# Graph attention and mixture of experts on one core: the transposes of a job's activations move between the two halves of an earlier job's second-layer product

## The reference, cut to what matters

```python
x = x + attention(layernorm(x), adj)        # 64 graphs, 128 nodes, 384 wide, 12 heads
u = layernorm(x)
logits = u.mean(nodes) @ router_w.T + router_b
top_v, top_i = top_k(logits, 2)             # 2 of 4 experts for each graph
gate = softmax(top_v)
h = act[e](u @ w1[e] + b1[e])               # act = gelu, silu, mish, gelu; 768 wide
out = h @ w2[e] + b2[e]
x = x + layernorm(gate-weighted sum of out + u)
```

## Time and profile before

| | |
|---|---|
| median of 3 runs | 1624.33 us (1623.05 to 1624.53) |
| the profiled execution's own time | 1624.39 us |
| its span in the trace | 1622.6 us |
| PE busy | 1587.3 us, 98% |
| DVE busy | 1195.4 us, 74% |
| ACT busy | 969.5 us, 60% |
| POOL busy | 686.8 us, 42% |
| matmul groups on L495 with `ut_in` (first layer) | x1536 and x768 |
| matmul groups on L495 with `at_hi`, `at_lo` (second layer) | x1524 and x762 |
| transposes on L709 | x768 |

### The profile page before, as it was taken

How to read it: one execution, slowest core, us unless ns; L and a number is a source line. 1 busy time by engine, 2 the same in 40 slices (tenths; PEclk the granted TensorE clock), 3 DMA queues, 4 the chain that set the end, 5 groups by cost and what they waited for, 6 DMA issues and landing times.

```text
span 1622.6 us, 44743 instructions
## 1 busy us (share of the span) xinstructions
PE 1587.3 (98%) x12720; PEld 1523.6 (94%) x12720; DVE 1195.4 (74%) x3754; ACT 969.5 (60%) x2880; POOL 686.8 (42%) x1105
## 2 busy tenths in 40 slices
PE   7999999999999999979999999999999999999998
PEld 7999999999999999869999999999999999999998
DVE  5787788878888788767766666776777767677776
ACT  6899999988889988853433333443444434343442
POOL 3777887778777787631111111111111111111112
PEclk9999999999999999999999999999999999999999
DMA  5433333344444433682111112211211111111211
GB/s 183 157 122 125 104 117 115 130 158 150 156 154 156 152 125 116 223 316 85 51 58 60 58 57 60 60 60 61 61 60 46 59 56 60 60 60 50 67 49 45
DMA packets 93511, 163.87 MB, mean 101 GB/s; under 512 B 10304, under 2 KB 73792, under 8 KB 92096
## 3 DMA queue, kind: packets, MB, share of 16 engines
q1 hardware_dynamic: 91664, 145.01, 27.3%
q10 hardware_dynamic: 1584, 15.73, 2.7%
HBM read 96.22 MB, written 64.49 MB: 99 GB/s over the span
## 4 chain that ended last, share of the span: by engine, by line
PE 89%; DVE 5%; ACT 2%; issue 2%; DMA 1%; DVEq 1%; POOL 0%; ACTq 0%; POOLq 0%; SPq 0%
PE bank L495 68%; PE bank L570 5%; PE bank L709 5%; PE bank L522 3%; PE bank L593 3%; PE bank L610 2%; PE bank L579 1%; PE bank L602 1%; DVE inverse L1461 1%; DVE half_t L1454 1%; DVE inverse L1457 1%; ACT inverse L1011 1%; ACT at_hi L1004 1%; DMA xu_scratch<-xu 1%; DVE hid L1335 0%
## 5 line engine op out<-in xcount | busy, mean ns | idle before, releaser
L495 PE MATMUL bank<-w_hi,ut_in 128*128 x1536 | 422.4, 342 | 0.4 <-issue 0.4
L495 PE MATMUL bank<-w_both,at_hi 128*128 x1524 | 388.6, 335 | 6.9 <-DVE at_lo L1426 6.2
L781 ACT ACTIVATE prob<-att,heads 128x128 f32<-128x128 f32 x768 | 297.7, 398 | 13.0 <-DVE heads L1178 10.8
L495 PEld LDWEIGHTS bank<-w_both,at_hi 128*128 128x128 f32 x1524 | 274.1, 188 | 12.5 <-issue 12.5
L495 PEld LDWEIGHTS bank<-w_hi,ut_in 128*128 128x128 f32 x1536 | 280.4, 189 | 1.4 <-issue 1.4
L495 PE MATMUL bank<-w_lo,ut_in 128*128 x768 | 257.6, 335 | 0.0
L495 PE MATMUL bank<-w_both,at_lo 128*128 x762 | 255.0, 335 | 0.0
L926 ACT ACTIVATE hid<-hid 128x384 f32<-128x384 f32 x192 | 95.0, 526 | 261.1 <-DVE hid L1335 256.2
L1004 ACT ACTIVATE at_hi<-bank,gate_col 128x384 fp32r<-128x384 f32 x254 | 133.7, 577 | 190.9 <-PE bank L709 189.0
L1154 POOL TENSOR_TENSOR xz<-xz,lnb_wide 128x384 f32<-128x384 f32 x64 | 68.0, 1063 | 405.9 <-DVE xz L1492 383.3
L1426 DVE SCALAR_TENSOR_TENSOR at_lo<-bank,gate_col,at_hi 128x384 fp32r<-128x384 f32 x254 | 144.7, 611 | 112.2 <-ACT at_hi L1004 112.2
(11 more groups left out here) (139 smaller groups left out, 3484.8 us busy)
## 6 DMA issues: line engine op xcount, KB each, us to landing
xu_scratch<-xu SPq DMA_DIRECT2D x64, 384.0 KB, 2.3
xz<-xu_scratch SPq DMA_DIRECT2D x64, 384.0 KB, 3.3
x_in<-in_x SPq DMA_DIRECT2D x32, 384.0 KB, 3.3
xu<-in_x SPq DMA_DIRECT2D x32, 384.0 KB, 4.4
ut_scratch<-ut_out SPq DMA_DIRECT2D x64, 192.0 KB, 1.9
ut_in<-ut_scratch SPq DMA_DIRECT2D x64, 192.0 KB, 2.3
out_dram<-xz SPq DMA_DIRECT2D x64, 192.0 KB, 1.9
w_lo<-in_L_ffn_w SPq DMA_DIRECT2D x4, 1152.0 KB, 6.6
```

The costliest lines, as they stand in the source:

```text
L495: last = nc.tensor.matmul(acc, lhs[c][a], rhs[c][b], start=start and n == 0, stop=stop and n == len(terms) - 1)
L781: nc.scalar.activation(prob[g][:, hh, :], att[g][:, head, :], ACT.Exp, bias=neg_max[g][:, head:head + 1], scale=-1.0, accum_out=row_sum[g] ...
```

## The change

In the second stage, PE's order becomes: at job j the first-layer product of j, the first half of the second-layer product of j - 2, the transposes of j - 1, the second half of the second-layer product of j - 2. ACT's second `at_hi` piece waits until the second-layer product of the job in front is over, since it overwrites what that reads. The transposes of the last job stand between the halves of job 126's product. The value loads that choose the experts (`choice`, L627) now stand one ahead of each product.

`half_t` moves to the memory of tiles `ot1` and `ot_hi1`, whose last reader is the last output projection (for which ACT waits there anyway), and `xz0` takes its place over `xu0`. ACT's wait for `xu_stored[0]` moves behind the activation of job 0, into the MISH branch of graph 0, ahead of the write of `miss2`.

In the first stage `transpose_probs` waits for one quadrant more with each piece and no longer for all four, and POOL does `root2(h - 3)` first in its last two steps, h = 62 and 63.

```diff
         at_lo = sb("at_lo", [P, FC, N], F32R)
+        xz = [sb("xz0", [P, 2, D])]
+        miss2 = sb("miss2", [P, 2, HALF])
+        xz.append(sb("xz1", [P, 2, D]))
+        b2_wide = sb("b2_wide", [P, E, D])
         half_t = sb("half_t", [P, 2, HALF])
-        miss2 = sb("miss2", [P, 2, HALF])
-        xz = [sb("xz0", [P, 2, D])]
-        b2_wide = sb("b2_wide", [P, E, D])
-        xz.append(sb("xz1", [P, 2, D]))
...
             def transpose_probs(n, c):
                 reached(pe, exp_done, HEADS * n + HPB * (c + 1))
-                reached(pe, max_done, QUAD * min(n + 2, B))
+                reached(pe, max_done, QUAD * (n + 1) + c + 1 if has(n + 1) else QUAD * B)
...
-            def second_layer(b, k, m, e):
+            def second_layer(b, k, m, e, s):
...
-                if k == 0:
+                if k == 0 and s == 0:
                     reached(pe, z_added, b - 1)
...
-                for s in range(2):
-                    reached(pe, at_lo_done, 2 * i + s + 1)
...
+                reached(pe, at_lo_done, 2 * i + s + 1)
...
-                last.then_inc(y_mm, 1)
+                if s == 1:
+                    last.then_inc(y_mm, 1)
 
             def expert_step(b, m, lap):
                 for k in range(K):
-                    ahead = isinstance(b, int) and b == 0
-                    first_e = choice(b, k) if graph(b, 0) and not ahead else None
-                    if graph(b, -1):
-                        second_e = choice(b - 1, k)
-                        if not last_job(b - 1, k):
-                            transpose_act(b - 1, k)
-                        if last_job(b - 1, k + 1):
-                            transpose_act(b - 1, k + 1)
-                    if graph(b, 0) and not ahead:
-                        first_layer(b, k, m, lap, first_e)
-                    if isinstance(b, int) and (b, k) == (1, 0):
-                        transpose_u(B - 1)
-                    if graph(b, -1):
-                        if isinstance(b, int) and b == 1 and k == 0:
-                            pe.wait_ge(w2_loaded, 16 * 6)
-                        second_layer(b - 1, k, m - 1, second_e)
-                    if isinstance(b, int) and (b, k) == (1, 0):
+                    first_e = choice(b, k) if 0 < b < B else None
+                    if first_e is not None:
+                        first_layer(b, k, m, lap, first_e)
+                    if (b, k) == (1, 0):
+                        transpose_u(B - 1)
+                        pe.wait_ge(w2_loaded, 16 * 6)
+                    if 0 < b <= B:
+                        second_e = choice(b - 1, k)
+                        second_layer(b - 1, k, m - 1, second_e, 0)
+                    if 0 < b <= B and k == 0:
+                        transpose_act(b - 1, 1)
+                    if b < B and k == 1:
+                        transpose_act(b, 0)
+                    if 0 < b <= B:
+                        second_layer(b - 1, k, m - 1, second_e, 1)
+                    if (b, k) == (1, 0):
                         logits(1)
...
             act.wait_ge(routed, 1)
             act.wait_ge(wo_mm, B)
-            for g in range(2):
-                act.wait_ge(xu_stored[0][g], 16 * stored(0))
             activate(0, 0, choice(0, 0))
...
                 for s in range(2):
+                    if s == 1:
+
+                        reached(act, y_mm, i)
                     nc.scalar.activation(flat(hi[:, s * DC:(s + 1) * DC, :]), banks[s][:, 0:HALF],
...
                     act.wait_ge(miss_done, i + 1)
+                    if isinstance(b, int) and b == 0:
+
+                        for g in range(2):
+                            act.wait_ge(xu_stored[0][g], 16 * stored(0))
                     nc.scalar.activation(miss2[:], half_t[:], ACT.Square, scale=-1.0, bias=one_col[:]).then_inc(miss2_done, 1)
...
             for h in range(STEPS.start, B):
+                if h >= B - 2:
+                    root2(h - 3)
...
-                if has(h - 3):
+                if has(h - 3) and h < B - 2:
                     root2(h - 3)
```

More of the change, by code:

```diff
@@ L727, in second_layer @@
-                last.then_inc(y_mm, 1)
+                reached(pe, at_lo_done, 2 * i + s + 1)
+                chunks = range(s * DC, (s + 1) * DC)
+                last = split_product(y_ps[m % 2][:, 0:D], [(hi[:, c, :], lo[:, c, :]) for c in chunks],
+                                     [tuple(w.rearrange("p e c d -> p (e c d)")[:, bass.ds(e * (FC * D) + c * D, D)]
+                                            for w in (w2_both[:, 1], w2_both[:, 0])) for c in chunks],
+                                     start=k == 0 and s == 0, stop=k == K - 1 and s == 1)
```

## The result

The changed kernel takes **1630.23 us** (median of 7 runs, 1628.47 to 1632.02); the kernel before, on the same chip, 1624.53 (7 runs, 1623.05 to 1626.18). The ratio is 1.0034, 95% interval 1.0023 to 1.0046: slower by 5.7 us. Forecast were 1631.3 us and slower.

The account below looks back on a forecast made before the run. PE was taken to bound the kernel, so only its idle stretches count. MISH 7.8, start -3.8, end -.5 and clock 3.4 sum to +6.9 us on 1624.4: 1631.3 us, range 1626.0 to 1636.0.

Parts of the forecast that it names:

- Place 1: Expert stage, 17 MISH jobs: transposes due 1.56 us sooner, their chain only .14, so PE waits; net +7.8 us.
- An isolated one: A MISH job without a MISH neighbour: PE idle 1.00 us before its transposes, 1.11 us in all, ten times.
- the chain's end: MISH chain's first half done at +9.02 us, counted from `take_hidden`, with PE starting the transposes at +9.16.
- A pair: Two neighbouring MISH jobs, the second waiting for the first's chain on DVE: 3.68 us per pair, three pairs.
- Place 2: Between the stages: norms and job 1's tanh come sooner, its transposes 6.2 us sooner; gain 3.8 us.
- over 2 us in hand: Between the stages: the last load of w2 moves up like the store, with over 2 us to spare.
- Place 3: End of the kernel: job 126's splits no longer follow bare on its transposes; gain .5 us (0 to 1.1).
- The clock: PE's clock halves after long gaps, one fall at the start and one among three MISH pairs: +3.4 us.
- Rival 1: PE's clock stays up, so the sum lacks the 3.4 us: 1627.9 us; chance .20.
- Rival 2: At the start the 6.2 us gain stays whole, with one clock fall: +2.8 us, 1627.2 us; chance .12.
- Rival 3: The MISH chain moves with the transposes, ending below +8.02, no isolated job stalls: -15.9 us, 1608.5 us; chance .05.
- Rival 4: Cutting the accumulation costs PE a second break, .09 us in each of 127 jobs: 11 us, 1642 us; chance .08.

Follow-up runs that it names:

- experiment 1: The changed kernel with the transposes moved back behind the whole product of the job in front, except those of jobs 126 and 127: 1620.45 us.
- experiment 6: Filler matmuls ahead of the second transposes of each MISH pair: eleven on the changed kernel, 1627.63 us; nine on the kernel cut after 4 chunks, 1621.38 us.
- experiment 3: The changed kernel with the product cut after 4 of its 6 chunks instead of 3, last jobs excepted: 1625.55 us.
- experiment 2: The changed kernel with the product cut after 5 of its 6 chunks instead of 3, last jobs excepted: 1618.32 us.

## Why the prediction was right

**Place 1, the MISH chain.** The mechanism is confirmed: ACT's squares hold `at_hi`, the chain gains a quarter of a microsecond while the transposes are due 1.56 us sooner, and PE is idle in front of them in all 16 later MISH jobs. An isolated one was put at 1.00 us idle and 1.11 in all; PE started .90 us after it was due, of which the profile shows .73 as idle, since the last matmul ends .17 behind the place of the next; the interval up to its transposes is 7.80 us and the next one .12 over 6.90, 1.02 in all. The mis-sized step is the chain's end: forecast at +9.02, measured at +8.34 + .55 = +8.90. I had `at_hi` start at the end of the squares, +3.53, as if one instruction began when the one before ended; it starts at +3.42: 1016.13 in the timeline, where the last square ends at 1015.29 + .94 = 1016.23. The two overlap by .1 us. A pair cost about 3.6 us, forecast 3.68. Sum 21.0 instead of 22.1, net +6.7 instead of +7.8. What the term rests on is shown three times: by removing MISH (sign reversed), by moving the cut (12.2 to 20.9 us, depending on the place), and by the waits.

**Place 2, the start.** Forecast 3.8 us, measured 3.8 (its terms as written, 6.2 - 1.56 - .7, give 3.9; measured are 6.1 - 2.3); norms at 693.7 against 692.22, tanh of job 1 at 715.4 against 715.24, its transposes at 724.9 against 724.97. The norms were sooner by 1.5 us and nothing came of it, as the exps behind them started at 694.15, after 1.21 us of idle time; the prediction had named what they wait for as due near 694.1. They came 3.55 us sooner than before (697.70), where 3.4 was forecast. I had the store of u transposed down as a possible loss of 1 us; ACT stood idle .35 us for it at 719.40. That the last load of w2 had "over 2 us in hand" is nearly so in the changed kernel: it landed at 719.15, job 0's half product ran from 720.05 to 723.10, and PE then waited 1.87 us for job 1. It does not hold in other combinations: in experiment 1 w2 landed at 721.05 and held the transposes of job 1 by .8 us, and with the layout alone it landed at 723.98. That the loads of the expert numbers are covered is right for the plain jobs, whose period stayed 6.90, and wrong behind the wait for w2, where one took .90 us.

**Place 3, the end.** .5 forecast, .5 measured. From the chain that ended last:

```profile
1613.30 0.16 issue
1613.46 1.85 PE bank L495 x9
```

The bare wait ahead of 1610.23 is gone, and a gap of .16 remains.

**The clock.** Forecast 3.4 us, one fall at the start and one in three pairs. In the profiled run it was 1.7, one fall behind the first pair: the interval from those transposes to the next is 8.59 us, behind the second pair, which had no fall, 7.02. The fall at the start is there (720.29, for 3.41 us) but lies over job 0's half product, of which the transposes of job 1 are independent; PE would have waited for them in any case. In the median of runs it was more: the fillers of experiment 6 put the pairs at one and a half to two and a half falls on average, not one. The total of 1631.3 against 1630.23 is right within the spread, but that close it is in part luck, for mis-sized terms partly cancel in it: MISH 1.1 us too high, the pairs' clock 1 to 2.5 us too low, the start's clock up to 1.7 too high. How many falls the start has on average was not measured.

**The rivals.** Rival 1 (no falls) is excluded for the median by the granted clocks and by experiment 6. Rival 2 (start 6.2 us) is refuted by 737.89 against 741.69. Rival 3 named +8.02 as the point that decides, and the chain ended at +8.90. Rival 4 fell with the period of 6.90 and with the kernel without MISH. Whether the quadrant waits do anything at the very end of the attention stage was not tried alone; root2 first accounts for ACT's gap without them.

## What to carry to other kernels

To move a consumer earlier in an in-order engine takes slack from its longest producer and gives it to its product; ask which of the two has none. Here the chain had .56 us in hand and the move was 1.56, and a cut two chunks later kept the gain without the loss. A wait written ahead of a register load uncovers the load: here .90 us. Where a wait of TensorE can't be removed, cheap matmuls in it may pay for themselves, and runs of one kernel that lie several microseconds apart are a reason to look at the granted clock behind each wait of TensorE.

## What was unexpected of the hardware

TensorE's clock fell behind waits as short as 1.9 us in the expert stage (experiment 3) and 1.8 us between the stages (1.84 with `root2` first alone, 1.81 in the second profile of the changed kernel), not only behind the 2.50 us of before. It depended on the run: the first pair's wait of 2.29 us was followed by a fall in one profile of the changed kernel and the same wait of 2.28 us in another was not; of twelve traced waits of 1.9 to 2.3 us in pairs four were. Each fall seen behind a pair lasted about 3.4 us at .50 and cost 1.6 to 1.7 us, half of that. The mean granted clock of an execution, rounded to .001, was enough to sort executions of one kernel by their falls. Behind waits of up to 1.4 us in the steady part of the expert stage (experiment 2's pairs) no profile here has one. The Trainium skill (TensorE: Matmul & The Clock Gate, HAM oscillation) warns there only of longer idle gaps than these; the runs don't agree. One fall cost nothing, as it lay over work that nothing waited for.
